# A two-layer recurrent and attention kernel: the start of the first layer put in another order, and its sine computed on GpSimd

## The chip, the cores and the metric

One core of one Trainium2 chip runs the kernel. The metric is the device time in microseconds (us). The kernel before took 806.47 us, the median of 3 runs (805.55 to 806.91). The engines are TensorE (PE), VectorE (DVE), ScalarE (ACT), GpSimd (POOL) and the DMA queues, of which SyncE (SP) issues nearly all. They run side by side and wait for one another on semaphores.

## The reference

The input is 16 sequences of 256 tokens with 256 features. Two layers follow; each is `x + s * silu(f)`, with `s` from a mixing branch and `f` from a feed-forward branch, both of the normalised `x`. All the changed instructions belong to layer 0:

```
xn = layernorm(x)
mag = exp(-exp(softplus(nu_log)));  theta = exp(theta_log)
A = mag * (cos(theta) + i sin(theta));  gamma = sqrt(1 - mag^2)
h[t] = A * h[t-1] + gamma * (xn[t] @ B)          # 32 complex states
s = Re(h @ C) + D * xn
f = gelu(xn @ proj1.T + b1) @ proj2.T + b2       # 256 -> 1024 -> 256
x = x + s * silu(f)
```

Layer 1 has attention with 16 heads in the place of the recurrence, and a linear layer with low-rank experts in the place of the MLP.

## The kernel before

Layer 0 works on 8 chunks of 512 rows (2 sequences). A float32 matmul is made of three products of rounded parts: each operand is split into a high part, written by ScalarE with a Copy (`xh`, `w1h`, `hh`), and the rest, a subtraction on VectorE (`xl`, `w1l`, `hl`). `three` (L505) issues low weight by high data, high weight by low data, high by high.

Every engine runs its own loop over the same steps `g` from 0 to 69, and within a step in the order in which the code stands; nothing is reordered at run time. Step g of TensorE is:

- up(g) (`l0_up`): 6 matmuls of 512 columns, block g % 8 of the hidden layer of chunk g // 8. ScalarE then makes GELU(g) and `hh` (L884), VectorE makes `hl` (`h_low`, L1317).
- down(g-2) (`l0_down`): 12 matmuls of 256 columns. They need `hh` and `hl` of block g-2, and two blocks share one quarter of `w2h` and `w2l`.
- At some steps also: the transposes of the next chunk, 4 matmuls a half (`l0_turn(c, 0)` and `l0_turn(c, 1)`); the input product of the recurrence (`l0_bu`); and its output product (`l0_y(c, b)`), at L777 to L813.

Both halves of the transposes of a chunk go through one bank, so `l0_turn(1, 1)` waits until ScalarE and VectorE have split the first half (L518 to L520: `xth` and `xtl` of 3). VectorE's split of it is `x_low(1, 0)`, which stands at the end of its step.

VectorE has in its steps: the splits of the weights (`w1_low`, `w2_low`), the norm of chunk 1 (`l0_norm(1)`, a generator of which `go` runs some pieces in each step), `magnitude` (from `nu_log` to `mag` and `gamma`: 31 instructions on one column, nearly all dependent; 23 at step 4 ahead of its `hl`, 8 at step 5), the recurrence `scan(c)` (10 instructions), `l0_sum` (adds the bias once all the down products of a chunk are there), `skip` and `states_out`.

GpSimd makes the powers of the rotation: exp(theta), the reduced angles of 1, 2, 4, ..., 128 steps, their sines and cosines, a table `CS` of 256 steps by doubling, and out of it `tci` and `tsi`, which `scan` reads, and `RR`, the signed output matrix that `l0_y` reads. The sines are taken by ScalarE (`angles`, L905), so GpSimd waits for ScalarE and ScalarE for GpSimd.

Of the kernel before, what the change touches and what calls it, by code (L numbers as in the profile page):

```python
# [56 lines left out]
GATE_REST = 9  # L57
L0_STEPS = 70
# [11 lines left out]
    "w1h", "w2h", "bh", "xth", "gelu", "hsh", "sin", "th0", "wrh", "wnh", "wmh", "lbh", "woh",  # L70
# [6 lines left out]
    "clean", "par", "ang", "nu", "tab", "rt", "fill", "rl", "lr", "kr", "kvr", "n", "qq", "nw", "rs", "oc", "kwk", "kwv",  # L77
# [94 lines left out]
def build(nc, x, consts, rows, vecs, w1t, w2t, b1c, bt, ct, nuth, wqn, wkbt, wqr, wkva, wvbt, wo,  # L172
          baset, lorab, loraa, routert, out):
    ctx = ExitStack()
    with ctx:
        SEM = {name: ctx.enter_context(nc.semaphore(name)) for name in SEMAPHORES}

        def sb(name, shape, dt=F32, where=ctx):
            return where.enter_context(nc.sbuf_tensor(name, shape, dt))
# [61 lines left out]
        VEC0 = sb("VEC0", [128, OFF_BB], F32, l0)  # L241
        l0.close()
# [93 lines left out]
        def col(i, n=1):  # L336
            return par[:, i:i + n]
# [164 lines left out]
        def _(e):  # L502
# [255 lines left out]
            for g in range(L0_STEPS):  # L758
# [16 lines left out]
                if g < 8 * NC:  # L775
                    l0_up(g // 8, g % 8)
                if g in (5, 12, 20, 28, 36, 44, 52, 60):  # L777
                    c = (5, 12, 20, 28, 36, 44, 52, 60).index(g)
                    l0_bu(c)
                if g in (10, 14, 22, 30, 38, 46, 54, 62):  # L780
                    c = (10, 14, 22, 30, 38, 46, 54, 62).index(g)
                    l0_y(c, 0)
# [28 lines left out]
                if g in (11, 16, 23, 31, 39, 47, 55, 63):  # L811
                    c = (11, 16, 23, 31, 39, 47, 55, 63).index(g)
                    l0_y(c, 1)  # L813
# [51 lines left out]
        def _(e):  # L865
            w = Waits(e, SEM)

            def w1_high(n):
                sl = slice(256 * n, 256 * n + 256)
                w.wait_ge(f"wu{n}", 16)  # L870
                e.activation(w1h[:, :, sl], st3[:, :, sl], ACT.Copy).then_inc(SEM["w1h"], 1)

            def w2_high(n):
                sl = slice(2 * n, 2 * n + 2)
                w.wait_ge(f"wd{n // 2}", 16)
                e.activation(w2h[:, sl, :], st8[:, sl, :], ACT.Copy).then_inc(SEM["w2h"], 1)
# [27 lines left out]

            def angles():  # L905
                w.wait_ge("ang", 1)
                w.wait_ge("sin", 1)
                e.activation(col(48, 16), col(32, 16), ACT.Sin).then_inc(SEM["sin"], 1)
# [139 lines left out]
            e.activation(col(56), tsn[:, 0:1], ACT.Sin).then_inc(SEM["sin"], 1)  # L1048
# [3 lines left out]
            for g in range(L0_STEPS):  # L1052
# [12 lines left out]
                if g == 3:  # L1065
                    b_high()
                if g == 0:
                    w1_high(1)
                if g == 0:
                    w1_high(2)  # L1070
                if g == 0:
                    w1_high(3)
# [4 lines left out]
                if g == 0:  # L1077
                    angles()
                if g == 1:
                    w2_high(0)  # L1080
                if g == 2:
                    w2_high(1)
                if g == 3:
                    w2_high(2)
                if g == 5:
                    w2_high(3)
# [27 lines left out]
                c, r = divmod(g - 4, 8)  # L1114
                if r == 0 and 0 <= c < NC - 1:
                    x_high(c + 1, 0)
# [58 lines left out]
        def _(e):  # L1175
# [148 lines left out]
            def scan(c):  # L1324

                w.wait_ge("bu", c + 1)
                w.wait_ge("tab", 3)
# [291 lines left out]
            for g in range(L0_STEPS):  # L1619
# [9 lines left out]
                if g == 1:  # L1629
                    w2_low(0)  # L1630
                if g == 2:
                    w2_low(1)
                if g == 3:
                    w2_low(2)
                if g == 6:
                    w2_low(3)
# [8 lines left out]
                if g == 0:  # L1645
                    w1_low(1)
                if g == 0:
                    w1_low(2)
                if g == 0:
                    w1_low(3)  # L1650
                if g in (9, 12, 20, 28, 36, 44, 52, 60):
                    c = (9, 12, 20, 28, 36, 44, 52, 60).index(g)
# [21 lines left out]
                if g == 0:  # L1674
                    norm = l0_norm(1)
                go(norm, 4)
# [14 lines left out]
                c, r = divmod(g - 4, 8)  # L1691
                if r == 0 and 0 <= c < NC - 1:
                    x_low(c + 1, 0)
# [88 lines left out]
        def _(e):  # L1782
# [50 lines left out]

            w.wait_ge("nuth", 16)
# [12 lines left out]
            w.wait_ge("par", done[0])  # L1847
            e.tensor_scalar(ab, r8, 0.5, None, ALU.mult, ALU.bypass).then_inc(SEM["ang"], 1)
# [3 lines left out]
            s8, c8, w8, v8 = col(48, 8), col(56, 8), col(32, 8), col(40, 8)  # L1852
            w.wait_ge("sin", 2)
            tt(c8, c8, c8, ALU.mult)
            ts(c8, c8, -2.0, 1.0, ALU.mult, ALU.add)
            tt(w8, s8, s8, ALU.mult, free=True)
            tt(v8, c8, c8, ALU.mult)
            tt(w8, w8, v8, ALU.add)
            ts(w8, w8, -0.5, 1.5, ALU.mult, ALU.add)
            tt(s8, s8, w8, ALU.mult)  # L1860
            tt(c8, c8, w8, ALU.mult, free=True)
            ts(v8, s8, -1.0, 1.0, ALU.mult, ALU.mult)
# [289 lines left out]
```

## Time and profile before

| | |
|---|---|
| median of 3 runs | 806.47 us |
| the profiled execution's own time | 806.92 us |
| its span (first to last instruction) | 805.1 us |
| PE busy | 785.2 us, 98% |
| DVE, ACT, POOL busy | 700.0, 523.6, 467.9 us |
| mean granted clock of TensorE | 0.991 |

The own time is 1.8 us above the span and 0.45 us above the median. "Busy" of PE counts matmuls that overlap, with modelled ends, so 98% says that it rarely stands still. In a timeline row the first number is the start, the second how long the row's instructions took; a value in brackets is how long the engine was idle before, and what ended that.

### The profile page before, as it was taken

The page shows a single profiled execution, that of the slowest core. Times are in us where ns is not written, and L with a number is a line of the kernel's source. Part 1 is how long each engine was busy: PE and PEld are TensorE (multiplying, and loading weights), DVE is VectorE, ACT ScalarE, POOL GpSimd, SP SyncE. Part 2 cuts the span into 40 slices and gives each one's busy share as a digit, 9 for nine tenths or more (in the row PEclk, how much of TensorE's full clock was granted, in tenths as well). Part 3 has the DMA queues.
Part 4 walks back from the last instruction along what each step waited for, and adds up shares of the span by engine and source line. Part 5 has one row for each costly group of instructions (what it writes and reads, how often), then busy time and mean ns, then how long its engine had stood idle before and what let it go on. Part 6 is the DMA issues. An engine that isn't in the chain of part 4 may idle for free.

```text
span 805.1 us, 23026 instructions
## 1 busy us (share of the span) xinstructions
PE 785.2 (98%) x7912; PEld 719.0 (89%) x7912; DVE 700.0 (87%) x2647; ACT 523.6 (65%) x1612; POOL 467.9 (58%) x1245
## 2 busy tenths in 40 slices
PE   7999999999999899999999999999999999999978
PEld 5988999888889799899989999999899998999957
DVE  6898787887787799899999999989999899998975
ACT  4554454444553687777767777777777777777672
POOL 6833022012334676866768667686776867759653
PEclk9999999999999899999999999999999999999999
DMA  8610012000001322232222322222232223312210
GB/s 305 239 34 1 1 66 67 1 0 2 1 14 28 59 42 46 49 52 53 53 39 44 56 53 53 37 46 49 53 61 36 46 42 57 64 34 48 45 38 29
DMA packets 101333, 41.15 MB, mean 51 GB/s; under 512 B 91744, under 2 KB 98400, under 8 KB 100576
## 3 DMA queue, kind: packets, MB, share of 16 engines
q1 hardware_dynamic: 98896, 38.89, 21.6%
q8 instruction: 63, 1.03, 0.5%
q10 hardware_dynamic: 2320, 0.79, 0.4%
q14 instruction: 54, 0.44, 0.2%
HBM read 14.47 MB, written 4.19 MB: 23 GB/s over the span
## 4 chain that ended last, share of the span: by engine, by line
PE 85%; DVE 5%; POOL 3%; issue 2%; SPq 2%; ACT 1%; DMA 1%; ACTq 0%; POOLq 0%; DVEq 0%
PE bank L507 57%; PE bank L713 11%; PE bank L735 8%; PE bank L706 3%; PE bank L571 1%; SPq L472 1%; PE bank L621 1%; POOL par L1790 1%; PE bank L581 1%; DVE QA L1521 1%; PE bank L524 1%; DMA QT<-QA 1%; DVE SM L1550 1%; DVE PT L1572 1%; SPq L403 1%
## 5 line engine op out<-in xcount | busy, mean ns | idle before, releaser
L1004 ACT ACTIVATE SM<-SM,stb 128x32 f32<-128x32 f32 (+7 forms) x512 | 206.1, 404 | 65.5 <-DVE stb L1550 62.1
L1951 POOL TENSOR_SCALAR SM<-SM,stb 128x32 f32<-128x32 f32 (+7 forms) x512 | 195.5, 400 | 79.4 <-DVE stb L1557 77.8
L507 PE MATMUL bank<-yh,wq_lo 128*128 128x256 f32 x512 | 151.4, 296 | 0.2 <-DVE QA L1521 0.2
L507 PE MATMUL bank<-yh,wq_hi 128*128 128x256 f32 x512 | 145.2, 284 | 0.0
L507 PE MATMUL bank<-yl,wq_hi 128*128 128x256 f32 x512 | 145.2, 284 | 0.0
L713 PE MATMUL bank<-KT,QT 128*128 128x192 f32 (+4 forms) x640 | 120.7, 327 | 1.7 <-DVE stb L1550 1.7
L1550 DVE CUSTOM_DVE_ANT_0 SM<-bank,CONST 128x224 f32<-128x224 f32 (+3 forms) x320 | 97.0, 346 | 22.4 <-PE bank L713 19.7
L713 PEld LDWEIGHTS bank<-KT,QT 128*128 128x128 f32 x640 | 97.6, 190 | 5.1 <-DVE stb L1550 3.4
L1572 DVE STREAM_TRANSPOSE PT<-SM 128x128 f32<-128x128 f32 (+2 forms) x232 | 99.4, 459 | 3.0 <-PE bank L735 2.7
L507 PEld LDWEIGHTS bank<-yh,wq_lo 128*128 128x128 f32 x512 | 97.7, 191 | 1.9 <-DVE QA L1521 0.4
L507 PEld LDWEIGHTS bank<-yl,wq_hi 128*128 128x128 f32 x512 | 97.7, 191 | 0.0
L507 PEld LDWEIGHTS bank<-yh,wq_hi 128*128 128x128 f32 x512 | 97.7, 191 | 0.0
L1004 ACT ACTIVATION_READ_ACCUMULATOR SM<-SM,stb 128x1 f32 x512 | 96.1, 188 | 0.0
L889 ACT ACTIVATE hs<-bank,B 128x512 f32<-128x512 f32 x64 | 43.9, 686 | 73.4 <-PE bank L507 68.1
L1944 POOL TENSOR_TENSOR QA<-QA 128x256 f32<-128x256 f32 x64 | 48.1, 751 | 71.2 <-DVE QA L1521 71.2
L1521 DVE TENSOR_TENSOR QA<-bank,TR 128x512 f32<-128x512 f32 x128 | 81.9, 681 | 4.5 <-DMA QT<-QA 3.8
L976 ACT ACTIVATE QT<-bank 64x512 f32<-64x512 f32 x128 | 75.3, 588 | 6.5 <-PE bank L507 5.0
L507 PE MATMUL bank<-woe_hi,ol 128*128 128x256 f32 x256 | 75.4, 295 | 0.6 <-DVE ol L1594 0.6
L507 PE MATMUL bank<-w2h,hl 128*128 128x256 f32 x256 | 74.3, 290 | 0.5 <-DVE w2l L1293 0.5
L507 PE MATMUL bank<-w2h,hh 128*128 128x256 f32 x256 | 72.3, 283 | 0.0
L507 PE MATMUL bank<-w2l,hh 128*128 128x256 f32 x256 | 72.3, 283 | 0.0
L507 PE MATMUL bank<-woe_hi,oh 128*128 128x256 f32 x256 | 72.1, 282 | 0.0
(215 smaller groups left out, 2081.0 us busy)
## 6 DMA issues: line engine op xcount, KB each, us to landing
QT<-QA SPq DMA_DIRECT2D x248, 64.0 KB, 2.1
PT<-KV SPq DMA_DIRECT2D x256, 16.0 KB, 1.8
out<-fo SPq DMA_DIRECT2D x32, 128.0 KB, 2.0
X<-in_x SPq DMA_DIRECT2D x7, 512.0 KB, 10.9
stage<-in_wqn SPq DMA_DIRECT2D x2, 1024.0 KB, 9.7
stage<-in_wo SPq DMA_DIRECT2D x2, 1024.0 KB, 5.0
stage<-in_w1t SPq DMA_DIRECT2D x4, 256.0 KB, 5.3
stage<-in_w2t SPq DMA_DIRECT2D x2, 512.0 KB, 6.6
```

What stands on the lines that cost most here:

```text
L507: i = e.matmul(dst, a, b, start=(first and j == 0), stop=(last and j == 2), skip_group_check=skip)
L706: j = e.matmul(sbank[n % 2][32 * i:32 * i + 32, at:to], KT[b % 3][:, p, 32 * kb:32 * kb + 32], Q[:, :, kb:3, i, :], start=True, stop=True)
L713: j = e.matmul(sbank[n % 2][:, at], Q[:, q, :, :].rearrange("p h c -> p (h c)"), KT[b % 3][:, p, 0:32 * q + 32], start=True, stop=True)
L735: j = e.matmul(sums[64 * half:64 * half + 64, :, 32 * q:32 * end], C[rows_, kb // 2, at], PT[rows_, 2 * half:2 * half + 2, kb, q:end, :], ...
L889: e.activation(hs[g % 2][:, :], fbank[g % 2][:, :], ACT.Gelu, bias=B1[:, g % 8:g % 8 + 1]).then_inc(SEM["gelu"], 1)
L976: i = e.activation(QT[r, (2 * b + g // 2) % 3, p, :, g % 2:4:2, :].rearrange("p n j c -> p j n c"), src[r, :, :, :], ACT.Copy)
L1004: i = e.activation(M[:, at], M[:, at], ACT.Exp, bias=S[:, 0, j:j + 1], scale=-1.0, accum_out=S[:, 1, j:j + 1])
L1521: i = e.tensor_tensor(QA[:, part, :, :, g % 2, :], src, TR[:, part, :].rearrange("p (n c) -> p n c", n=8).unsqueeze(1).broadcast_to([128, ...
L1550: i = e.tensor_tensor_reduce(M[:, at], bk[:, at], mask[:, 224 - 32 * q:256], 1.0, 3e38, ALU.add, ALU.min, S[:, 0, j:j + 1])
L1572: return e.transpose(PT[:, slot, 0:k, q:q + some, :].rearrange("p k q c -> p q k c"), src)
L1944: e.tensor_tensor(A[:, 0, 0, :, :], A[:, 0, 0, :, :], A[:, 1, 1, :, :], ALU.subtract)
L1951: i = e.tensor_scalar(P[:, at], P[:, at], S[:, 2, j:j + 1], 1.0, ALU.mult, ALU.mult)
```

## The change

1. The Sin activation is gone from ScalarE. In its place GpSimd evaluates a polynomial (of degree 6 in the square of the half angle, for sine and cosine in one tile `trig`). ScalarE's first activation is a GELU on one column, whose result is not used.
2. `RR` is signed after `tci` and `tsi`; the scan waits for 2 tables, and `l0_y` for all 3.
3. The first up product, `l0_first`, has its four products with `xh` first and those with `xl` last.
4. The splits of w1's later quarters move from step 0 to steps 0, 2 and 4, those of w2 from steps 1, 2, 3, 5 (6 on VectorE) to 1, 3, 5, 6; the split of B on ScalarE moves from step 3 to 4.
5. The norm of chunk 1 starts at step 2 and ends at step 4 (it was step 0 to 2); the first half of chunk 1 is transposed and split at step 5 and no longer at 4.
6. The recurrence of chunk 0 moves from step 9 to 10 on VectorE (its output products on TensorE from 10 and 11 to 11 and 12); that of chunk 1 from 12 to 13 (14 to 15).

```diff
+TURN_FIRST = (5, 12, 20, 28, 36, 44, 52)
+            def l0_first():
+                sl = slice(0, 128)
+                w.wait_ge("w1h", 1)
+                w.wait_ge("w1l", 1)
+                for k in range(2):
+                    w.wait_ge("xth", k + 1)
+                    e.matmul(fbank[0][:, :], w1l[:, k, sl], xh[0][:, k, :], start=(k == 0), stop=False)
+                    e.matmul(fbank[0][:, :], w1h[:, k, sl], xh[0][:, k, :], start=False, stop=False)
+                for k in range(2):
+                    w.wait_ge("xtl", k + 1)
+                    i = e.matmul(fbank[0][:, :], w1h[:, k, sl], xl[0][:, k, :], start=False, stop=(k == 1))
+                i.then_inc(SEM["f1"], 1)
...
             def l0_y(c, b):
+                w.wait_ge("tab", 3)
                 w.wait_ge("zz", 2 * c + b + 1)
...
-                if g in (5, 12, 20, 28, 36, 44, 52, 60):
+                if g in (5, 13, 20, 28, 36, 44, 52, 60):
                     l0_bu(c)
-                if g in (10, 14, 22, 30, 38, 46, 54, 62):
+                if g in (11, 15, 22, 30, 38, 46, 54, 62):
                     l0_y(c, 0)
...
-            e.activation(col(56), tsn[:, 0:1], ACT.Sin).then_inc(SEM["sin"], 1)
+            e.activation(trig[:, 15, 0:1], tsn[:, 0:1], ACT.Gelu)
...
-                if g == 0:
-                    angles()
...
-                w.wait_ge("tab", 3)
+                w.wait_ge("tab", 2)
...
-                if g in (9, 12, 20, 28, 36, 44, 52, 60):
+                if g in (10, 13, 20, 28, 36, 44, 52, 60):
                     go(make)
                     scan(c)
...
-                if g == 0:
+                if g == 2:
                     norm = l0_norm(1)
-                go(norm, 4)
+                go(norm, {2: 1, 3: 4}.get(g, 9))
...
-                c, r = divmod(g - 4, 8)
-                if r == 0 and 0 <= c < NC - 1:
+                if g in TURN_FIRST:
+                    c = TURN_FIRST.index(g)
                     x_low(c + 1, 0)
...
+            s8, c8, v8 = col(48, 8), col(56, 8), col(40, 8)
+            ts(ab, r8, 0.5, None, ALU.mult)
+            both = ab.unsqueeze(1).broadcast_to([128, 2, 8])
+            tt(q1.rearrange("p (i n) -> p i n", i=2), both, both, ALU.mult)
+            tt(SUMS[:, 0:3, :], ODD, q1.unsqueeze(1).broadcast_to([128, 3, 16]), ALU.mult)
+            tt(q2, q1, q1, ALU.mult, free=True)
+            tt(SUMS[:, 0:3, :], SUMS[:, 0:3, :], EVEN, ALU.add)
+            tt(q4, q2, q2, ALU.mult, free=True)
+            tt(PAIRS, SUMS[:, 1:4:2, :], q2.unsqueeze(1).broadcast_to([128, 2, 16]), ALU.mult)
+            tt(PAIRS, PAIRS, SUMS[:, 0:3:2, :], ALU.add)
+            tt(q1, PAIRS[:, 1, :], q4, ALU.mult)
+            tt(q1, q1, PAIRS[:, 0, :], ALU.add)
+            tt(r8, r8, q1[:, 0:8], ALU.mult)
+            tt(s8, r8, q1[:, 8:16], ALU.mult)
+            tt(c8, r8, r8, ALU.mult, free=True)
+            ts(c8, c8, -0.5, 1.0, ALU.mult, ALU.add)
+            ts(v8, s8, -1.0, 1.0, ALU.mult, ALU.mult, free=True)
```

TensorE's first up product before, behind the transposes (`xh0` and `xl0` are the parts of chunk 0, `w1h` and `w1l` those of the weight):

```order
L524 MATMUL bank<-CONST,xn0 128x128 x8
L507 MATMUL bank<-xh0,w1l 128x512
L507 MATMUL bank<-xl0,w1h 128x512
L507 MATMUL bank<-xh0,w1h 128x512
L507 MATMUL bank<-xh0,w1l 128x512
L507 MATMUL bank<-xl0,w1h 128x512
L507 MATMUL bank<-xh0,w1h 128x512
```

The same place in the changed kernel:

```order
L527 MATMUL bank<-CONST,xn0 128x128 x8
L539 MATMUL bank<-xh0,w1l 128x512
L540 MATMUL bank<-xh0,w1h 128x512
L539 MATMUL bank<-xh0,w1l 128x512
L540 MATMUL bank<-xh0,w1h 128x512
L543 MATMUL bank<-xl0,w1h 128x512 x2
```

Both products with `xl0` now stand last of the six.

VectorE before, from step 4 (the last `hl` of the first part of `magnitude`) to step 6; `xl1` is the split of chunk 1, the first one `x_low(1, 0)`, the second `x_low(1, 1)`:

```order
L1321 TENSOR_TENSOR hl1<-hs0,hh1 128x512
L1314 TENSOR_TENSOR xl1<-bank,xh1 128x512
L1201 SCALAR_TENSOR_TENSOR par<-par,pari 128x1
L1196 TENSOR_TENSOR par<-par 128x1
L1198 TENSOR_TENSOR par<-par 128x1
L1201 SCALAR_TENSOR_TENSOR par<-par 128x1
L1196 TENSOR_TENSOR par<-par 128x1
L1198 TENSOR_TENSOR par<-par 128x1
L1201 SCALAR_TENSOR_TENSOR par<-par 128x1
L1280 TENSOR_TENSOR par<-par 128x1
L1321 TENSOR_TENSOR hl2<-hs1,hh2 128x512
L1293 TENSOR_TENSOR w2l<-stage1,w2h 128x512
```

The same place in the changed kernel:

```order
L1325 TENSOR_TENSOR hl1<-hs0,hh1 128x512
L1297 TENSOR_TENSOR w2l<-stage1,w2h 128x512
L1205 SCALAR_TENSOR_TENSOR par<-par,pari 128x1
L1200 TENSOR_TENSOR par<-par 128x1
L1202 TENSOR_TENSOR par<-par 128x1
L1205 SCALAR_TENSOR_TENSOR par<-par 128x1
L1200 TENSOR_TENSOR par<-par 128x1
L1202 TENSOR_TENSOR par<-par 128x1
L1205 SCALAR_TENSOR_TENSOR par<-par 128x1
L1284 TENSOR_TENSOR par<-par 128x1
L1325 TENSOR_TENSOR hl2<-hs1,hh2 128x512
L1318 TENSOR_TENSOR xl1<-bank,xh1 128x512
```

`x_low(1, 0)` has gone behind a weight split, the second part of `magnitude` and one more `hl`.

VectorE before, around the first recurrence (`hl2` is the split of block 8, the four `G` and `g3` begin the scan, `z0` is `l0_sum`, `xn0` is `skip`):

```order
L1321 TENSOR_TENSOR hl2<-hs0,hh2 128x512
L1333 TENSOR_TENSOR G<-bank,tci 64x256
L1334 TENSOR_TENSOR G<-bank,tsi 64x256
L1333 TENSOR_TENSOR G<-bank,tci 64x256
L1334 TENSOR_TENSOR G<-bank,tsi 64x256
L1336 TENSOR_TENSOR g3<-G 128x256
L1338 SCALAR_TENSOR_TENSOR gs<-par,g3 128x256
L1344 TENSOR_TENSOR Z0<-gs,CS 64x256
L1345 TENSOR_TENSOR Z0<-gs,CS 64x256
L1344 TENSOR_TENSOR Z1<-gs,CS 64x256
L1345 TENSOR_TENSOR Z1<-gs,CS 64x256
L1369 TENSOR_TENSOR z0<-bank,VEC0 128x512 x2
```

The same place in the changed kernel:

```order
L1325 TENSOR_TENSOR hl2<-hs0,hh2 128x512
L1373 TENSOR_TENSOR z0<-bank,VEC0 128x512 x2
L1325 TENSOR_TENSOR hl0<-hs1,hh0 128x512
L1357 TENSOR_TENSOR xn0<-xn0,VEC0 128x512
L1337 TENSOR_TENSOR G<-bank,tci 64x256
L1338 TENSOR_TENSOR G<-bank,tsi 64x256
L1337 TENSOR_TENSOR G<-bank,tci 64x256
L1338 TENSOR_TENSOR G<-bank,tsi 64x256
L1340 TENSOR_TENSOR g3<-G 128x256
```

`l0_sum`, the `hl` of block 9 and the second `skip` now come ahead of the scan.

## Rows read from the trace of the kernel before

**Rows 1.** The page: busy time of each engine.
```profile
PE 785.2 (98%) x7912; PEld 719.0 (89%) x7912; DVE 700.0 (87%) x2647; ACT 523.6 (65%) x1612; POOL 467.9 (58%) x1245
```

**Rows 2.** The timeline of TensorE: start, length, line, operands, [idle before, releaser].
```profile
11.45 0.47 PE L507 MATMUL bank<-xh,w1l 128*128 128x512 f32 x1 [1.14 <-DVE xl L1314]
...
17.60 0.47 PE L507 MATMUL bank<-xh,w1l 128*128 128x512 f32 x1 [1.59 <-ACT hs L889]
...
28.66 0.39 PE L507 MATMUL bank<-xh,bl 128*128 128x512 f32 x1
...
31.46 0.40 PE L507 MATMUL bank<-xh,w1l 128*128 128x512 f32 x1
...
32.85 0.60 PE L524 MATMUL bank<-CONST,xn 128*128 128x128 f32 x4
...
45.28 1.13 PE L571 MATMUL bank<-RR,Z 128*128 128x256 f32 x4 [0.56 <-DVE Z L1345]
...
62.04 0.63 PE L524 MATMUL bank<-CONST,xn 128*128 128x128 f32 x4 [0.79 <-DVE xl L1314]
```

**Rows 3.** The timeline of ScalarE, start of the first layer.
```profile
15.47 1.28 ACT L889 ACT_TABLE_LOAD   x1
...
17.49 0.63 ACT L893 ACTIVATE hh<-hs 128x512 fp32r<-128x512 f32 x1
```

**Rows 4.** The timeline of VectorE, up to 47 us.
```profile
10.61 1.29 DVE L1314 TENSOR_TENSOR xl<-bank,xh 128x512 fp32r<-128x512 f32 x2 [0.63 <-ACT xh L882]
...
14.48 1.40 DVE L1212 BATCH_NORM_STATS2 st<-X 128x6 f32<-128x256 f32 x4
...
17.20 0.19 DVE L1201 SCALAR_TENSOR_TENSOR rs<-rs,ri 128x4 f32<-128x4 f32 x1
...
18.25 0.69 DVE L1321 TENSOR_TENSOR hl<-hs,hh 128x512 fp32r<-128x512 f32 x1 [0.86 <-ACT hh L893]
...
25.33 0.14 DVE L1245 TENSOR_SCALAR par<-par 128x1 f32<-128x1 f32 x1
...
29.55 0.69 DVE L1321 TENSOR_TENSOR hl<-hs,hh 128x512 fp32r<-128x512 f32 x1
30.16 0.68 DVE L1314 TENSOR_TENSOR xl<-bank,xh 128x512 fp32r<-128x512 f32 x1
...
32.26 0.73 DVE L1321 TENSOR_TENSOR hl<-hs,hh 128x512 fp32r<-128x512 f32 x1
...
41.38 0.41 DVE L1333 TENSOR_TENSOR G<-bank,tci 64x256 f32<-64x256 f32 x1
...
46.15 1.29 DVE L1369 TENSOR_TENSOR z<-bank,VEC 128x512 f32<-128x512 f32 x2
```

**Rows 5.** TensorE's granted clock in stretches: length, busy times, clock (before DMA share), GB/s.
```profile
12.00:15.00 3.00, 3.00 (x8) 2.32 (x7) 2.25 (x5) 0.66 (x2) 2.49 (x7) 0.50 1.06 398
...
275.00:281.40 6.40, 5.78 (x44) 5.34 (x45) 4.29 (x28) 1.44 (x7) 3.14 (x8) 0.50 0.51 97
...
769.50:772.80 3.30, 2.79 (x48) 2.30 (x48) 2.04 (x17) 1.13 (x6) 1.07 (x3) 0.52 0.16 50
16.00:17.60 1.60, 0.01 (x1) 0.03 (x1) 1.22 (x10) 1.56 (x3) 1.13 (x6) 1.00 1.00 415
```

**Rows 6.** The timeline of TensorE at its two longest waits.
```profile
275.62 1.51 PE L706 MATMUL bank<-QT,KT 128*32 128x192 f32 x24 [2.97 <-DVE stb L1550]
...
769.59 2.79 PE L706 MATMUL bank<-QT,KT 128*32 128x192 f32 x48 [2.54 <-DMA QT<-QA]
```

**Rows 7.** The timeline of GpSimd: begin of the sines, one long row, the last table.
```profile
20.74 0.69 POOL L1796 TENSOR_TENSOR par<-par 128x8 f32<-128x8 f32 x1
...
23.09 2.37 POOL L1790 TENSOR_SCALAR par<-par 128x8 f32<-128x8 f32 x1
...
25.99 0.20 POOL L1790 TENSOR_SCALAR par<-par 128x8 f32<-128x8 f32 x1
...
40.37 0.55 POOL L1875 TENSOR_SCALAR tsi<-CS,par,CONST 128x256 f32<-128x256 f32 x1
```

More of the change, by code:

```diff
@@ L1 @@
+import math
 from contextlib import ExitStack
@@ L241, in build @@
         VEC0 = sb("VEC0", [128, OFF_BB], F32, l0)
+        trig = sb("trig", [128, 16, 16], F32, l0)
         l0.close()
@@ L774, in _ @@
                     l1_tk(0, wbank)
-                if g < 8 * NC:
+                if g == 0:
+                    l0_first()
+                elif g < 8 * NC:
                     l0_up(g // 8, g % 8)
-                if g in (5, 12, 20, 28, 36, 44, 52, 60):
-                    c = (5, 12, 20, 28, 36, 44, 52, 60).index(g)
+                if g in (5, 13, 20, 28, 36, 44, 52, 60):
+                    c = (5, 13, 20, 28, 36, 44, 52, 60).index(g)
                     l0_bu(c)
-                if g in (10, 14, 22, 30, 38, 46, 54, 62):
-                    c = (10, 14, 22, 30, 38, 46, 54, 62).index(g)
+                if g in (11, 15, 22, 30, 38, 46, 54, 62):
+                    c = (11, 15, 22, 30, 38, 46, 54, 62).index(g)
                     l0_y(c, 0)
@@ L1064, in _ @@
                     gate_exp(0)
-                if g == 3:
+                if g == 4:
                     b_high()
-                if g == 0:
-                    w1_high(1)
-                if g == 0:
-                    w1_high(2)
-                if g == 0:
-                    w1_high(3)
+                if g in (0, 2, 4):
+                    w1_high(1 + g // 2)
                 if g == 65:
@@ L1076, in _ @@
                     y_high(0, wbank)
-                if g == 0:
-                    angles()
[L1079 to L1086, printed above, removed]
+                if g in (1, 3, 5, 6):
+                    w2_high((1, 3, 5, 6).index(g))
                 if g == 38:
@@ L1112, in _ @@
                     nope_high(1, 1)
-                c, r = divmod(g - 4, 8)
-                if r == 0 and 0 <= c < NC - 1:
+                if g in TURN_FIRST:
+                    c = TURN_FIRST.index(g)
                     x_high(c + 1, 0)
@@ L1628, in _ @@
                     l1_norm(1)
[L1629 to L1636, printed above, removed]
+                if g in (1, 3, 5, 6):
+                    w2_low((1, 3, 5, 6).index(g))
                 if g == 58:
@@ L1644, in _ @@
                     skip(c, 1)
[L1645 to L1650, printed above, removed]
-                if g in (9, 12, 20, 28, 36, 44, 52, 60):
-                    c = (9, 12, 20, 28, 36, 44, 52, 60).index(g)
+                if g in (0, 2, 4):
+                    w1_low(1 + g // 2)
+                if g in (10, 13, 20, 28, 36, 44, 52, 60):
+                    c = (10, 13, 20, 28, 36, 44, 52, 60).index(g)
                     go(make)
@@ L1690, in _ @@
                     h_low(g)
-                c, r = divmod(g - 4, 8)
-                if r == 0 and 0 <= c < NC - 1:
+                if g in TURN_FIRST:
+                    c = TURN_FIRST.index(g)
                     x_low(c + 1, 0)
@@ L1831, in _ @@
             done[0] += 1
+            ODD, EVEN, SUMS, PAIRS = (trig[:, i:i + n, :] for i, n in ((0, 3), (3, 3), (6, 4), (10, 2)))
+            q1, q2, q4 = (trig[:, i, :] for i in (12, 13, 14))
+            for k in range(7):
+                at = SUMS[:, 3, :] if k == 6 else (ODD if k % 2 else EVEN)[:, k // 2, :]
+                e.memset(at[:, 0:8], float((-1) ** k / math.factorial(2 * k + 1)))
+                i = e.memset(at[:, 8:16], float((-1) ** k / math.factorial(2 * k)))
+            i.then_inc(SEM["par"], 1)
+            done[0] += 1
             w.wait_ge("nuth", 16)
```

36 lines of the change are left out of this document (9 added, 27 removed).

## The prediction

> **What bounds the kernel now.** I read the busy time by engine first, then the timelines of the four engines over the first 70 us, since every changed instruction runs there. TensorE is busy for 98% of the span [rows 1], so what follows the start is a belt of matmuls: a microsecond that TensorE gains or loses in its first steps is a microsecond at the end, if nothing gives it back on the way. The reader is to look for TensorE's waits. At the start there are 1.14 us for the low part of x, and 1.59 us for the first GELU at 17.60 [rows 2], which the exchange of ScalarE and GpSimd over the sines had held back: the Sin came first and then a load of the GELU table, 1.28 us [rows 3]. Then TensorE stands twice for VectorE: 0.56 us at 45.28 for the first recurrence, and 0.79 us at 62.04 for the split of chunk 2 [rows 2]. The second thing to see is VectorE. It runs without a gap from 18.25 to 33.5 [rows 4], and runs behind TensorE: TensorE is at the input product of step 5 at 28.66 [rows 2] when VectorE has yet to write a split of step 4, `x_low(1, 0)`, at 30.16 [rows 4]. TensorE needs it at 32.85 [rows 2]. So TensorE's cover there is 32.85 - 30.8 = 2.0 us. That number decides this change.
>
> **The first steps: what is saved.** With the products on `xh` first, TensorE need not wait for `xl`: `xh` is there when VectorE begins its `xl` at 10.61 [rows 4], so the first product starts at 10.65 and not 11.45. The last product waits for the second `xl` (11.90) and ends at 12.35. ScalarE's GELU(0) follows at 12.4, with no Sin and no table load between; before it began at 15.47 + 1.28 = 16.75 [rows 3]. So ScalarE's chain starts 4.3 us earlier. It then has GELU, `hh`, the w2 copy, GELU and `hh`: by rows 3 a GELU takes 0.72 (17.49 less 16.77) and a copy 0.55 to 0.6, so `hh(1)` is there at 12.4 + 2 x 0.72 + 3 x 0.55 = 15.5. TensorE gets ahead by about 3 us: its wait at 17.60 and most of the slow stretch at 12 to 15 go.
>
> **VectorE: what the saved time meets.** From `hl(0)` at 18.25 to the first instruction of `magnitude` at 25.33 it works without a gap for 7.08 us [rows 4]. The new order, from `hl(1)` at 15.5, has three pieces less (`hl(0)` and two w2 splits, 0.61 each by 29.55 to 30.16 [rows 4]) and two w1 splits more (1.22), and the statistics of chunk 1 with the first round of the root, 14.48 to 17.39 = 2.91 us, which before ran in the shadow of the wait for the Sin. That is 7.08 - 1.83 + 1.22 + 2.91 = 9.4 us, and `magnitude` begins at 24.9: only 0.4 us earlier. Its 23 instructions take 29.55 - 25.33 = 4.22 us [rows 4], to 29.1. Then, before, came one `hl` and `x_low(1, 0)`. Now `x_low(1, 0)` stands at step 5, behind `hl` (0.6), a w2 split (0.6), the rest of `magnitude` (30.76 to 32.26 = 1.5, the 30.76 being 30.16 + 0.6 [rows 4]), and another `hl` (0.6): it begins at 32.4 and ends at 33.1.
>
> TensorE, meanwhile, is held at step 5 by the split of B, which ends at 24.9. From there it has the input product and the down product (28.66 to 31.46 = 2.80 [rows 2]), the first transposes (0.35) and up(6) (31.46 to 32.85 = 1.39), and stands before `l0_turn(1, 1)` at 29.45. It waits there for `x_low(1, 0)` until 33.15: **3.7 us idle, and 0.3 us later than before** (32.85). The whole gain of the start is spent. Both ends of this term: if the clock falls as at 12 to 15 [rows 5], up(1) takes 1.2 us longer and `hl(1)` comes 0.65 us later, which makes +0.95; if VectorE's pieces are shorter by what GpSimd's smaller share of blocked reads might save, 0. I take +0.3, as the gap ahead of the first product is now 0.3 us where 1.14 went ahead of the slow stretch.
>
> **The recurrence a step later.** From the transposes to the end of down(7) TensorE has no wait: 43.15 before (0.35 + 1.43 + 3 steps of 2.82 from 32.85), 43.45 now. Before, VectorE filled the time between `hl(8)` and that end with the scan (41.38 to 46.15 [rows 4]). Now `l0_sum`, which needs down(7), stands ahead of it, so VectorE idles from 41.4 to 43.5, whatever the offset: up(8) frees its `hl` 2.1 us after its end, down(7) ends 4.25 us after it. Then two sums, an `hl` and a `skip` (4 x 0.6 = 2.4) to 45.9, and the scan gives its first product 45.28 - 41.38 = 3.9 us later [rows 2, 4]: 49.8. TensorE arrives, after up(10), down(8) and up(11), at 43.45 + 4.2 = 47.65 and waits 2.15 us. The same work (up(11) and the first output product) was done at 49.1 before, at 50.55 now: +1.45. A part comes back, since VectorE then sets the pace: it has 7.2 us of work (six instructions at 0.6, the norm of chunk 2 at 1.3, the rotary weights' split at 2.3) from the scan's end (50.7) to the sum of states that frees the bank of `l0_bu(1)`, 57.9, where TensorE waits some 0.4 us; the 0.79 us at 62.04 (1.1 if one goes by the starts of rows, as the 0.56 is 0.75; ends of matmuls are modelled) is gone, because `x_low(2, 0)` is now early. Net over the stretch: 2.15 + 0.4 - 0.75 - 1.1 = +0.7; with rounding of the starts I put **+0.6**. From below this is 0 (VectorE catches up in its later gaps), from above 1.45.
>
> **The clock.** Here the trace of before is the witness. After 2.97 us and after 2.54 us idle [rows 6] TensorE resumed at a granted clock of 0.50, which is 1.2 and not 2.4 GHz, and kept it until 281.4 and 772.8 [rows 5]: 5.8 and 3.2 us of work at half speed. After 1.14 us idle, with gaps ahead of that, 3.2 us were at half (12.0 to 15.2); after 1.59 us none (1.00 at 16.00:17.60 and after). A wait of 3.7 us is longer than any of these, so I expect 3.2 to 5.8 us at half speed behind it, a loss of 1.6 to 2.9 us. Two of the three rows say the smaller: **+1.6**. It is on the path: down(7) comes later by as much.
>
> **GpSimd.** The 14 memsets run while it waits for its first input. One instruction fewer ahead of `magnitude`'s input, 15 where 9 were for the sines: 6 more at 0.3 us is +1.8, less the 0.3, and `RR` behind `tci` and `tsi` gives 0.5 back. The last table that the scan needs was ready at 40.92 [rows 7]; now at about 41.9. The scan starts at 45.9, so this costs nothing; the cover is 4 us. What GpSimd shows of contention: a row of 8 columns takes 0.20 us at 25.99 but 2.37 us from 23.09 to 25.46 [rows 7], while VectorE ran `hl`, split, `hl`, split.
> The Trainium skill (SBUF — State Buffer, "Who interferes with whom") says that a VectorE instruction with two SBUF inputs blocks a GpSimd instruction that reads SBUF for its whole length; this row agrees. By that rule each of the six extra instructions could meet such a run; that is the rival of the late table below. By the rule as by the row the sum stays as it is until 4 us of cover are used up.
>
> **Sum.** 0.3 + 0.6 + 1.6 = +2.5 us on 806.92, the profiled execution's own time: 809.4. The median of the runs is 0.45 below that execution, so 809.0 for the median. Its own range: 0 + 0 + 1.6 to 0.95 + 1.45 + 2.9, which is +1.6 to +5.3, 808.0 to 811.8.
>
> **Rivals.**
> 1. *The waits come, the clock does not fall.* For it: 1.59 us idle left the clock at 1.00. Against: both waits above 2.5 us lowered it. Time: +0.9, 807.4. Chance 22%.
> 2. *Faster: the start's gain gets through.* One mechanism: `x_low(1, 0)` ends before TensorE stands at the second transposes. Then TensorE goes on at 29.5, not 32.85: -3.4, and +0.6 for the scan: -2.8, 803.7. It decides when VectorE is 3.6 us ahead of my sum at that place; any lead below 0.3 us gives nothing. Against it: 17.6 us of packed VectorE work whose pieces all have rows. For it: I may misplace a wait of VectorE in the old order that does not come back in the new one; half the lead would be -1.1 and no fallen clock. Chance 15%, mostly between 803.7 and 805.5.
> 3. *The table becomes the bound.* If GpSimd's sines and doublings take 4 us more than I put, each further microsecond moves the scan and the end. Two blocked rows like that at 23.09 (2.2 us extra each) on top would do it. With 1 us beyond: +3.5, 810.0. Chance 5%.
> My forecast has 58%.
>
> **Chances.** A measurement of this kernel can tell about 0.2%, 1.6 us. Slower by more: the forecast's 58% save its lowest edge, and the late table: 0.60. Within: the first rival and the edges: 0.26. Faster: 0.14. The range leaves out most of the second rival and the top of the third: 805.3 to 811.3.
>
> **What would show it.** In the new profile: ScalarE's first GELU at 12.4 with no table load before it; TensorE's first product at 10.65; `magnitude` at 24.9 and the split `xl` of chunk 1 at 32.4; a TensorE wait of 3 to 4 us that ends at about 33 with transposes, and a granted clock of 0.5 behind it; VectorE idle 2 us before `l0_sum`; a wait of about 2 us at the first output product. The prediction is wrong if `xl` of chunk 1 comes before 31, if no TensorE wait above 1.5 us stands between 20 and 40 us, or if the second table ends after 45.

## The result, and the profile after

The changed kernel takes 809.02 us, the median of 11 runs (807.03 to 813.27), against 806.2 for 11 runs of the kernel before, taken in turns on the same chip: a ratio of 1.004, 95% interval 1.0023 to 1.0058. It is slower by about 3 us. The forecast was 809.0.

The two profiled executions do not show it at first sight. The one of after has a span of 805.2 us and an own time of 807.03, which is the fastest of its 11 runs; the one of before has 805.1 and 806.92. What has to be compared is where each stands on the way, and at which clock. The page's line of the busy engines:

```profile
PE 781.3 (97%) x7912; PEld 715.3 (89%) x7912; DVE 700.8 (87%) x2647; ACT 522.0 (65%) x1610; POOL 467.5 (58%) x1264
```

TensorE is busy 3.9 us less than in [rows 1] in the same span: it stands still more, and runs less at half clock. The mean granted clock is 0.998, before 0.991. Windows of after (start:end, us, busy time and count by engine, granted clock, DMA share, GB/s) over the stretches that answer to [rows 5]:

```profile
12.00:15.00 3.00, 3.00 (x14) 2.36 (x13) 1.55 (x3) 2.40 (x4) 2.41 (x8) 1.00 1.07 392
33.70:39.70 6.00, 5.98 (x40) 5.52 (x41) 3.56 (x6) 1.92 (x3) 5.45 (x13) 1.00 0.64 218
277.90:281.90 4.00, 4.00 (x39) 3.55 (x40) 3.68 (x22) 1.35 (x6) 1.98 (x6) 0.59 0.75 141
```

Before had three slow stretches (12, 275 and 769.5); this execution has one, at 278. The timeline of TensorE (start, duration, line, operation, count; in brackets how long it had stood and for whom) answers to [rows 2]:

```profile
10.72 0.47 PE L539 MATMUL bank<-xh,w1l 128*128 128x512 f32 x1 [0.34 <-ACT xh L903]
15.46 0.36 PE L510 MATMUL bank<-w2h,hl 128*128 128x256 f32 x1 [0.20 <-DVE w2l L1297]
25.52 0.47 PE L510 MATMUL bank<-xh,bl 128*128 128x512 f32 x1 [1.36 <-DVE bl L1303]
33.72 0.63 PE L527 MATMUL bank<-CONST,xn 128*128 128x128 f32 x4 [3.32 <-DVE xl L1318]
50.68 1.10 PE L590 MATMUL bank<-RR,Z 128*128 128x256 f32 x4 [2.23 <-DVE Z L1349]
58.89 0.50 PE L510 MATMUL bank<-xh,bl 128*128 128x512 f32 x1 [0.18 <-DVE xn L1364]
71.57 1.02 PE L590 MATMUL bank<-RR,Z 128*128 128x256 f32 x4
```

The last row is the last output product of chunk 1, a place that comes behind everything that was moved. The kernel before is there 1.99 us earlier. Its first down product and that last output product:

```profile
19.69 0.36 PE L507 MATMUL bank<-w2h,hl 128*128 128x256 f32 x1 [0.46 <-DVE w2l L1293]
69.58 1.02 PE L571 MATMUL bank<-RR,Z 128*128 128x256 f32 x4
```

The first down product is at 15.46 where it was at 19.69, so the start did bring 4.2 us. It is all gone at 33.72: there the kernel before, at 32.85, is ahead by 0.87. VectorE shows why (answering to [rows 4]):

```profile
15.78 0.71 DVE L1325 TENSOR_TENSOR hl<-hs,hh 128x512 fp32r<-128x512 f32 x1 [0.46 <-ACT hh L914]
25.29 0.15 DVE L1249 TENSOR_SCALAR par<-par 128x1 f32<-128x1 f32 x1
32.89 0.68 DVE L1318 TENSOR_TENSOR xl<-bank,xh 128x512 fp32r<-128x512 f32 x1
44.28 1.29 DVE L1373 TENSOR_TENSOR z<-bank,VEC 128x512 f32<-128x512 f32 x2 [2.11 <-PE bank L510]
46.69 0.41 DVE L1337 TENSOR_TENSOR G<-bank,tci 64x256 f32<-64x256 f32 x1
```

From 15.78 to 33.5 no row of it shows a gap, and `magnitude` begins at 25.29, as before (25.33). ScalarE, in its timeline, has the load of the table at 1.18 us, where it hides behind the input's transfer, and GELU(0) at 12.56 where it was 16.77:

```profile
1.18 1.28 ACT L1064 ACT_TABLE_LOAD   x1 [1.18 <-PEq L2147]
12.56 0.69 ACT L910 ACTIVATE hs<-bank,B 128x512 f32<-128x512 f32 x1 [0.99 <-PE bank L543]
```

GpSimd, in its own timeline, has a group of 8 polynomial instructions (3.06 us from 22.39; the last of them is the first row here) and the second table of the recurrence; the table is ready at 41.48:

```profile
24.89 0.56 POOL L1790 TENSOR_TENSOR trig<-trig 128x16 f32<-128x16 f32 x1
40.93 0.55 POOL L1881 TENSOR_SCALAR tsi<-CS,par,CONST 128x256 f32<-128x256 f32 x1
```

### The profile page after: what moved, and what is told of

Same layout as the page of the kernel before. It is cut to its first block, busy times and chain, and to the rows that moved or that the text cites. A ratio compares the mean times of both kernels' runs of the same rounds, so it can differ in the third digit from the quotient of the medians.

```text
span 805.2 us, 23043 instructions
## 1 busy us (share of the span) xinstructions
PE 781.3 (97%) x7912; PEld 715.3 (89%) x7912; DVE 700.8 (87%) x2647; ACT 522.0 (65%) x1610; POOL 467.5 (58%) x1264
## 4 chain that ended last, share of the span: by engine, by line
PE 84%; DVE 7%; issue 2%; SPq 2%; POOL 1%; DMA 1%; ACT 1%; ACTq 0%; POOLq 0%; DVEq 0%
PE bank L510 57%; PE bank L732 11%; PE bank L754 8%; PE bank L725 3%; PE bank L590 2%; SPq L475 1%; PE bank L600 1%; PE bank L640 1%; DVE QA L1525 1%; DMA QT<-QA 1%; PE bank L527 1%; DVE SM L1554 1%; DVE PT L1576 1%; SPq L406 1%; PE bank L614 1%
```

## The experiments

Every kernel below was timed in turns with the kernel before, which stood at 805.95, 805.96 and 805.84 us (26, 35 and 35 runs) in the three sets of four (experiments 1 to 4, 5 to 8, 9 to 12), each set on another chip. "The mark" is the last output product of chunk 1 (69.58 before, 71.57 after).

**1. The changed kernel again**, for a second profile.

> The changed kernel itself, beside the others on one chip. The theory (two VectorE-bound waits at the start, 3.3 us ahead of the second transposes of chunk 1 and 2.2 us ahead of the first output product): the same two waits, TensorE 2.0 us later than before at the last output product of chunk 1 (71.6 against 69.6), and 809 us where before has 806 to 806.5. The rival (the difference of 2.8 us between the medians was a matter of when TensorE's clock fell in single executions): no difference to before in these rounds.

809.56 us, ratio 1.0053 (1.0037 to 1.007). Same code, same wait, another clock:

```profile
33.71 1.09 PE L527 MATMUL bank<-CONST,xn 128*128 128x128 f32 x4 [3.31 <-DVE xl L1318]
53.31 2.05 PE L590 MATMUL bank<-RR,Z 128*128 128x256 f32 x4 [2.23 <-DVE Z L1349]
75.28 1.02 PE L590 MATMUL bank<-RR,Z 128*128 128x256 f32 x4
```

```profile
33.70:39.70 6.00, 5.99 (x23) 5.48 (x24) 2.45 (x4) 0.60 (x1) 5.46 (x12) 0.51 0.63 218
53.40:56.60 3.20, 3.20 (x11) 2.84 (x12) 3.16 (x8) 0.00 (x0) 0.00 (x0) 0.50 0.00 0
```

In six microseconds TensorE gets 23 matmuls done instead of 40, and after the second wait it is slow again. The mark comes 3.7 us later than in the first profile. So the same program can lose 3.7 us on its first 75, or nothing.

**2. First transposes at step 4 again.**

```diff
-TURN_FIRST = (5, 12, 20, 28, 36, 44, 52)
+TURN_FIRST = (4, 12, 20, 28, 36, 44, 52)
```

> The changed kernel with only the first transposes and the split of chunk 1 back at step 4. The theory: TensorE then waits for the norm of chunk 1 at its first transposes (until 25.0, some 4 us), and the second transposes find the split there: they begin at about 32.4 and not 33.7, so the end comes 1.3 us sooner, 807.7. Rival (it is VectorE's total work up to that point that sets the time, wherever the split stands): unchanged, 809.

807.9 us, 1.0031 (1.0017 to 1.0045), where 807.7 was expected and the rival had 809. The long wait moved and did not go:

```profile
25.30 1.11 PE L527 MATMUL bank<-CONST,xn 128*128 128x128 f32 x4 [3.81 <-DVE xn L1229]
35.51 0.60 PE L527 MATMUL bank<-CONST,xn 128*128 128x128 f32 x4
52.43 1.10 PE L590 MATMUL bank<-RR,Z 128*128 128x256 f32 x4 [2.23 <-DVE Z L1349]
```

TensorE now stands for the norm of chunk 1 and not for its split, and the clock was at half from 24.3 to 31.9. The second transposes have no wait. The work from the first transposes to the end of the next up product takes 6.01 us here (25.30 to 31.31) and 3.25 in the kernel before (25.41 to 28.66), so half clock cost 2.8 us. Without it, as an estimate, the second transposes would stand at 32.7 and the mark at 70.6, 1.0 us ahead of the changed kernel. So the place of the split is worth about 1 us; the rest of the wait is VectorE's work ahead of the norm, wherever the transposes stand.

**3. The recurrence of chunk 0 at step 9 again.**

```diff
-                if g in (10, 13, 20, 28, 36, 44, 52, 60):
+                if g in (9, 13, 20, 28, 36, 44, 52, 60):
...
```

(and its output products at 10 and 11, on TensorE and VectorE alike)

> The changed kernel with only the first recurrence back at step 9 (its output products at 10 and 11). The theory: VectorE no longer idles 2.1 us before the bias sum, the scan starts at 42.2 behind the split of block 8 (the tables are there at 41.5), the wait at the first output product falls from 2.2 to about 0.6 us, and the last output product of chunk 1 comes 1.1 us sooner: 807.9. Rival (the table is the bound, which is why the scan was moved): the scan starts later than 43 and nothing is gained.

806.84 us, 1.002 (1.0007 to 1.0033), 2.7 us under the changed kernel in the same set. The second wait is gone:

```profile
33.68 0.63 PE L527 MATMUL bank<-CONST,xn 128*128 128x128 f32 x4 [3.32 <-DVE xl L1318]
47.60 1.10 PE L590 MATMUL bank<-RR,Z 128*128 128x256 f32 x4 [0.48 <-DVE Z L1349]
70.84 1.02 PE L590 MATMUL bank<-RR,Z 128*128 128x256 f32 x4
```

The clock was at half from 35 to 38.8 here, so the mark says too little; experiment 9 has it clean. The gain is more than double what I had expected (1.1).

**4. `magnitude` two steps later**, so that the split of chunk 1 comes ahead of it.

```diff
-                if g == 4:
+                if g == 6:
                     make = magnitude()
```

> The changed kernel with magnitude started at step 6 in place of 4, so that the split of chunk 1 does not stand behind it. The theory: no wait of TensorE at the second transposes, which begin at 30.3; the whole 3.4 us of the start reach the end, less what the clock does: 805.6 to 806. Rival (the 31 small instructions only move, and VectorE lacks the same 5.7 us a little later): at the first output product TensorE waits for what it gained, 809.

806.69 us, 1.0019 (1.0005 to 1.0032), where 805.6 to 806 was expected.

```profile
30.31 0.60 PE L527 MATMUL bank<-CONST,xn 128*128 128x128 f32 x4
48.07 2.04 PE L590 MATMUL bank<-RR,Z 128*128 128x256 f32 x4 [3.06 <-DVE Z L1349]
70.88 1.02 PE L590 MATMUL bank<-RR,Z 128*128 128x256 f32 x4
```

The transposes start 3.4 us earlier and without a wait: taking the 31 small instructions (4.2 and 1.5 us) from ahead of `x_low(1, 0)` is enough to end it. But the next wait grows from 2.23 to 3.06, which is 0.8 us, and the clock behind it is at half: from the first output product to the next transposes it is 5.33 us (48.07 to 53.40), where the changed kernel's first profile has 3.76 (50.68 to 54.44). At the mark 0.7 us is left of the 3.4. GpSimd's part in the wait, in its timeline (the last of the group of 8, and the second table):

```profile
24.98 2.37 POOL L1790 TENSOR_TENSOR trig<-trig 128x16 f32<-128x16 f32 x1
43.01 0.98 POOL L1881 TENSOR_SCALAR tsi<-CS,par,CONST 128x256 f32<-128x256 f32 x1
```

The table is ready 2.5 us later (43.99 where it was 41.48), and the recurrence starts at 44.07. Most of it is one instruction of 16 columns: it starts at 24.98 and takes 2.37 us, where the changed kernel has 24.89 and 0.56. VectorE now runs the split of B, `hl`, a split and `hl` back to back beside it (25.04 to 27.26), and it ends at 27.35. In the changed kernel instructions on one column follow the split of B, which ends at 25.37, and GpSimd's ends at 25.45.

**5. Unused matmuls in both waits**, of 512 columns each into a bank that nothing reads, 13 ahead of the second transposes and 8 ahead of the first output product, so that TensorE does not stand.

```diff
+                if (c, k) == (1, 1):
+                    for i in range(13):
+                        e.matmul(wbank[:, :], w1h[:, 0, 0:128], xh[0][:, 0, :], start=True, stop=True)
...
```

> The changed kernel with 13 matmuls of 512 columns into an unused bank ahead of the wait at the second transposes, and 8 ahead of the wait at the first output product; their results are used by nothing. They fill 2.8 of the 3.3 us and 1.7 of the 2.2 us. The forecast's theory (the clock falls behind the long wait in most executions and costs about 1.6 us): the median falls by 1 to 1.6 us against the changed kernel, to 807.5 to 808, and the mean granted clock rises. Rival (the clock does not fall there; the waits cost their own length only): the same median, 809.

807.68 us, 1.0019 (1.0004 to 1.0034), 1.9 us under the changed kernel in experiment 1; the mean granted clock over its 12 runs is 0.9966, over all 17 of the changed kernel 0.9942.

```profile
33.74 0.63 PE L530 MATMUL bank<-CONST,xn 128*128 128x128 f32 x4 [0.38 <-DVE xl L1324]
50.70 1.10 PE L596 MATMUL bank<-RR,Z 128*128 128x256 f32 x4 [0.42 <-DVE Z L1355]
71.61 1.02 PE L596 MATMUL bank<-RR,Z 128*128 128x256 f32 x4
```

The useful work is where it was to 0.04 us, and the granted clock was 1.00 over the first 70 us. What is left of the distance to the kernel before (1.7 us) is what the order of the work costs; what is gone fits the clock's share.

**6. Edits 3 and 4 together.**

> Both: magnitude at step 6 and the first recurrence at step 9. The theory: with TensorE 3.4 us ahead the tables (41.5) are the bound, the scan starts at 41.6 and not at 38.7, blocks the bias sum and the split behind it, and TensorE waits 3 us at the first output product; that is 0.9 us worse than magnitude at step 6 with the scan at 10, so about 806.7. Rival (the scan at 9 is better in any case, as with the changed kernel's start): 1 us better, 804.8.

808.17 us, 1.0029 (1.0015 to 1.0044): worse than either alone.

```profile
46.89 1.78 PE L590 MATMUL bank<-RR,Z 128*128 128x256 f32 x4 [4.76 <-DVE Z L1349]
71.70 1.02 PE L590 MATMUL bank<-RR,Z 128*128 128x256 f32 x4
```

With the recurrence early and its table late (ready at 42.80), VectorE stands 2.53 us at the table with two sums and an `hl` queued behind, and the wait is 4.76 us, followed by half clock from 47 to 50.7. The late table of the one edit meets the early recurrence of the other; I had the direction of that and not its size (806.7).

**7. The kernel before with the new sines alone** (`RR` last and the GELU table first go with them).

```diff
-                e.activation(col(48, 16), col(32, 16), ACT.Sin).then_inc(SEM["sin"], 1)
-            e.activation(col(56), tsn[:, 0:1], ACT.Sin).then_inc(SEM["sin"], 1)
+            e.activation(trig[:, 15, 0:1], tsn[:, 0:1], ACT.Gelu)
```

> The kernel before with the sines on GpSimd, the GELU table loaded at the start and RR signed last; all orders of before. The theory: GELU(0) at 13.8, the first split of VectorE at 17.4 behind the statistics of chunk 1 and not at 18.25, TensorE 0.85 us ahead until step 9; the scan then waits for the table (41.5) and TensorE for the scan, so almost nothing is left: 806.0, same. Rival (the exchange with ScalarE was the real cost at the start): 2 us faster, 804.3.

807.32 us, 1.0018 (1.0003 to 1.0033), 1.3 over the expectation. Its first down product is 0.4 us earlier than before's, its second transposes 0.4 us (32.44), and then:

```profile
45.97 1.10 PE L590 MATMUL bank<-RR,Z 128*128 128x256 f32 x4 [1.66 <-DVE Z L1349]
```

```profile
41.97 0.42 DVE L1337 TENSOR_TENSOR G<-bank,tci 64x256 f32<-64x256 f32 x1 [0.98 <-POOL tsi L1883]
```

Taking 1.28 us of table load off ScalarE brings nothing, since VectorE sets the pace there; and with the recurrence in its old place GpSimd's table is on the path, 0.98 us late (second fence, VectorE's timeline). At the mark it is 0.6 us behind the kernel before (70.18). This is the one use of moving the recurrence to step 10.

**8. The same with `l0_first`.**

> The same, and the first product in its new order. The theory: VectorE's first split still comes at 17.4, so TensorE's 0.8 us earlier start is hidden, same as the kernel without it, 806.0; only a clock that stays up at 12 to 15 could show, and that stretch lies in the shadow of VectorE. Rival: 0.8 us faster than the kernel with the sines alone.

806.54 us, 1.0008 (0.9997 to 1.0019): no difference from before. It is 0.8 us under experiment 7, as the rival had it, but the two intervals overlap, so that gain is not shown.

```profile
15.69 0.47 PE L510 MATMUL bank<-xh,w1l 128*128 128x512 f32 x1 [1.70 <-DVE w1l L1292]
20.02 0.55 PE L510 MATMUL bank<-w2h,hl 128*128 128x256 f32 x1 [2.71 <-DVE w2l L1299]
```

The first product is at 10.80, 0.65 us early, and the lead is lost at once for the splits of w1 and w2, which stand in the old order. Behind the 2.71 us the granted clock was 0.53 from 20.0 to 23.4.

**9. Edit 3 with the 13 unused matmuls of edit 5** (the recurrence at step 9, the wait at the second transposes filled; the 8 matmuls of edit 5 are not in it).

> The changed kernel with the first recurrence back at step 9 and 13 matmuls, used by nothing, in the wait at the second transposes. The theory (each wait costs its length, and the long one costs the clock besides): the recurrence at 9 without a fallen clock, 1 to 1.5 us below the kernel with the recurrence at 9 alone (806.8), so 805.6. Rival (the fill of both waits gained 1.9 us at the second wait only, which is small here): 806.8 again.

806.95 us, 1.002 (1.0002 to 1.0038): 1.3 us over the expectation, and no better than experiment 3. Its 12 times fall into two groups: six from 804.9 to 805.7 with mean granted clocks of 0.995 to 0.998, and six from 808.2 to 809.5 with 0.992 to 0.994. The median lies where no run is.

```profile
33.77 0.63 PE L530 MATMUL bank<-CONST,xn 128*128 128x128 f32 x4 [0.39 <-DVE xl L1321]
46.13 1.10 PE L593 MATMUL bank<-RR,Z 128*128 128x256 f32 x4 [0.45 <-DVE Z L1352]
69.37 1.02 PE L593 MATMUL bank<-RR,Z 128*128 128x256 f32 x4
```

At the mark it is 2.2 us ahead of the changed kernel and 0.2 ahead of the kernel before. Its profile has slow stretches later on, at 275 to 279 and 770 to 776, in code that no edit touches; the kernel before has such stretches at the same two places [rows 5].

**10. `magnitude` in two parts**: 3 pieces at step 4, none at step 5, the rest later.

```diff
-                go(make, 7)
+                go(make, {4: 3, 5: 0}.get(g, 7))
```

> The changed kernel with magnitude in three parts: 3 pieces at step 4, none at 5, the rest from 6. The split of chunk 1 comes at 29.7, TensorE does not wait at the second transposes (30.3), and VectorE's two-input instructions are less bunched than with magnitude at 6, so the tables are ready by 42.5 and not 44. The theory: first output product at 47.3 (48.1 with magnitude at 6), wait 2.3 us, last output product of chunk 1 at about 69.5 with the clock up; median 806.0. Rival (GpSimd's tables and its roots for chunk 2 are the bound once TensorE is 3 us ahead, whatever VectorE's order): the output product at 48, 806.7 as with magnitude at 6.

805.73 us, 1.0003 (0.9987 to 1.0019): the best variant, equal to the kernel before. The second transposes start at 30.19 without a wait, the table is ready at 41.85, and the profile's clock is 1.00 throughout:

```profile
47.37 1.10 PE L590 MATMUL bank<-RR,Z 128*128 128x256 f32 x4 [2.50 <-DVE Z L1349]
69.90 1.02 PE L590 MATMUL bank<-RR,Z 128*128 128x256 f32 x4
275.89 0.86 PE L725 MATMUL bank<-QT,KT 128*32 128x192 f32 x24 [2.97 <-DVE stb L1554]
```

```profile
275.30:282.80 7.50, 6.91 (x75) 6.75 (x76) 7.12 (x46) 5.08 (x25) 3.12 (x8) 1.00 0.45 85
```

**11. Experiment 10 with 8 unused matmuls ahead of the first output product.**

```diff
+                if (c, b) == (0, 0):
+                    for i in range(8):
...
```

> The same with 8 matmuls, used by nothing, ahead of the first output product. The theory: no slow stretch at 47 to 51, 1 to 1.5 us less in the median than without, 804.8, below both kernels. Rival (that wait is too short to matter): 806.

808.11 us, 1.0031 (1.0014 to 1.0047), over 3 us above the expectation.

```profile
47.34 1.10 PE L593 MATMUL bank<-RR,Z 128*128 128x256 f32 x4 [0.68 <-DVE Z L1352]
69.87 1.02 PE L593 MATMUL bank<-RR,Z 128*128 128x256 f32 x4
276.00 1.51 PE L728 MATMUL bank<-QT,KT 128*32 128x192 f32 x24 [2.97 <-DVE stb L1557]
```

```profile
275.30:282.80 7.50, 6.80 (x50) 6.35 (x51) 5.00 (x30) 2.46 (x10) 3.19 (x8) 0.54 0.44 84
```

The mark is where experiment 10 has it, to 0.03 us. Then both meet the same wait of 2.97 us at 276, and one goes on at full clock with 75 matmuls in 7.5 us, the other with 50. I have no reason for it in the first 70 us. Nor does the clock account for the 2.4 us between the medians: the mean granted clocks of the two sets of 12 runs are 0.9954 and 0.9947, and 0.0007 of the span is 0.6 us. The rest is open.

**12. Experiment 11 with GpSimd's rotary tables behind the roots for the norm of chunk 2.** In experiment 11 VectorE stood 1.54 us for these roots, and TensorE 1.12 us, at 52.4, for the norm.

```diff
+                if g == 8:
+                    w.wait_ge("const", 16)
+                    for q in range(2):
...
+                    i.then_inc(SEM["rt"], 1)
```

> The same, and GpSimd's rotary tables made behind the roots of chunk 2 and not ahead of them, so those roots are ready 1.4 us earlier. The theory: VectorE does not wait for them before the norm of chunk 2 (1.8 us with magnitude at 6), 0.5 us less, 804.3. Rival (that wait has cover in TensorE): the same as without.

806.53 us, 1.0013 (0.9996 to 1.0031), 2.2 us over the expectation.

```profile
68.38 1.02 PE L593 MATMUL bank<-RR,Z 128*128 128x256 f32 x4
768.14 2.79 PE L728 MATMUL bank<-QT,KT 128*32 128x192 f32 x48 [3.09 <-DMA QT<-QA]
```

At the mark it is 1.2 us ahead of the kernel before and 3.2 ahead of the changed one; the median is 0.7 above before. Late in the run, at the second row, it is still 1.45 us ahead (before: 769.59 [rows 6]). Then the clock is at 0.55 from 768 to 778.5, where before has half clock for 3.3 us, and the profile ends 1.9 us behind. No variant beat the kernel before by more than its interval.

## Why the prediction was right, step by step

**The start's gain is spent at the second transposes: right in mechanism, too small.** Forecast: first product at 10.65, GELU(0) at 12.4, `magnitude` at 24.9, the split of chunk 1 at 32.4, TensorE released at 33.15. Measured: 10.72, 12.56, 25.29, 32.89, 33.72. The wait is 3.32 us where I put 3.7. The term is +0.87 where I put +0.3, inside its bounds (0 to 0.95). `hl(1)` is at 15.78 and not 15.5, which is half of it; the rest is about 0.1 us in each of VectorE's packed stretches. Experiment 4 shows the cause by taking it away: without the 31 small instructions ahead the transposes start at 30.31. Experiment 10, which leaves 12 of them there, has 30.19. No run moves the later norm or the weight splits back alone, so what each of them adds to VectorE's packed work is argued from its rows and not shown.

**The scan a step later: mis-sized.** The wait at the first output product is 2.23 us (forecast 2.15), VectorE's idle time ahead of the sum 2.11 (2.1), and the later wait 0.18 (0.4). The net was to be +0.6 and is +1.12: 71.57 - 69.58 = 1.99, less 0.87. The step that failed is a subtraction in mixed measures: I took the two waits of before by the starts of rows (0.75 and 1.1) and those of after in the rows' own measure. In one measure it is 2.23 + 0.18 - 0.56 - 0.79 = +1.06. Experiments 3 and 9 say what this edit costs inside the new order: 2.7 us by the medians (experiment 3 against 1), 2.2 at the mark (9 against the profile after). That is double the 1.1: between the second transposes and the mark, step 9 in the new order is 1.1 us faster than step 9 in the old one (the other edits gain that much there), and the move to step 10 costs 2.2 from that.

**The clock: size about right, and not a fixed event.** Forecast: behind the wait of 3.7 us half clock for 3.2 to 5.8 us, +1.6. In the first profile the clock stayed at 1.00 behind 3.32 us; in the second it fell behind 3.31, and the mark was 3.7 us later. Over the 13 profiles that are not of the kernel before, TensorE had a wait of 2.7 us or more in the first 70 us seven times, and the clock was at half during it or just behind it in six; the exception is the first profile of after. The share in the median I can only estimate: each run's record has its mean granted clock, and a straight line of time over clock gives at full clock 806.4 for the 17 runs of after and 804.0 for the 96 of before (803.6 to 804.5 by set), a difference of 2.4. That is near the 1.99 of the mark. The mean of all 17 runs of after is 809.6, that of before 806.0; 3.6 less 2.0 to 2.4 leaves 1.2 to 1.6 us. The mean clocks themselves, 0.9942 and 0.9952, are only 0.001 apart, which is 0.8 us of the span. The estimate holds only if a part of before's half clock falls where TensorE waits anyway; the stretch at 12 to 15, ahead of its wait at 17.60, may be such a part, but no run measures it. Experiment 5 is the better witness: it takes 1.9 us away by filling the waits, with the useful work in place and a higher mean clock.

But experiments 9 and 11 filled a wait too and gained nothing, or lost, and their mean clocks are no higher for it (0.9951 against 0.9948 in experiment 3, 0.9947 against 0.9954 in experiment 10). The slow stretches at 275 and 770 are not theirs alone: behind the wait of 2.97 us at 275 to 281 the clock fell in 13 of all 14 profiles, before among them, and around 770, behind waits of 1.7 to 3.5 us, in 8. That it is chance which execution has them, and not the edit's doing, is not shown.

**GpSimd's table costs nothing: right.** It was ready at 41.48, forecast 41.9, needed at 46.69. The cover was real, though: at the old place of the scan it was 0.98 us late (experiment 7). The long row of [rows 7] comes again in experiment 4, as one instruction of 16 columns: 2.37 us there, 0.56 in the changed kernel. It ends 0.09 us after the last of four packed VectorE instructions in the one and 0.08 us after a single one in the other. The Trainium skill (SBUF — State Buffer, "Who interferes with whom") has a VectorE instruction with two SBUF inputs hold up GpSimd's reads for its length; the 1.8 us between these two rows agree with it, though here one GpSimd instruction stood through four of them, and no run varied VectorE's inputs alone.

**The rivals.** *Waits without a fallen clock* (807.4) is what the one profiled execution shows, with own time 807.03; the median of 11 is not there. *The start's gain gets through* (803.7) needed VectorE 3.6 us earlier at the split; experiment 4 gave it that, and still the median was 806.69: in its profile the next wait took 0.8 of the 3.4 us and the half clock behind it 1.6. That rival was priced too high even on its own condition. *The late table* did not come.

So the forecast of +2.5 is the order's 0.9 and the clock's 1.6. Measured it is 2.0 for the order, and 2.8 (medians of the first 11 runs) to 3.6 (means of all) in total. The two waits and the half clock behind them were forecast rightly, and the sum is inside its range on its merits; that 809.0 was met to 0.02 us is luck. The order was put 1.1 us too low (0.6 at the second transposes, 0.5 behind them, where the subtraction in mixed measures stands), the clock's 1.6 lies between the 0.8 that the first 11 medians leave for it (2.8 less 2.0) and the 1.9 of experiment 5, and the sum was set on 806.47, where more runs gave 806.0.

## What to carry to other kernels

When engines run fixed step orders, a lead is worth only what the next engine in the loop can follow: list the work that stands packed ahead of the instruction the bottleneck waits for, and count small dependent instructions by time (23 of them were 4.2 us here) before moving anything past them. Compare two profiles at a mark behind all moved work and at the same granted clock, in one measure of waiting for both; equal spans can hide 2 us, as they do here. If waits differ, take several profiles of the same kernel before a clock effect of a microsecond or two is put down to an edit.

## What the runs showed of the hardware that I had not expected

- The granted clock behind a wait is not settled by the wait's length. The same 3.3 us at 33.7 was followed by full clock in one execution and by 6 us at 0.51 in another; the same 2.97 us at 276 by 1.00 in experiment 10 and 0.54 in experiment 11.
- Over all 14 profiles the 2.97 us at 275 to 281 was followed by half clock 13 times; experiment 10 is the one exception.
- Shorter waits can do it too: behind 2.23 us the clock was at 0.50 for 3.2 us in experiment 1, and at 1.00 behind the same wait in the first profile of after.
- One program's runs spread over 6 us (807.03 to 813.27 for after, 803.52 to 809.84 for before), more than any edit here was worth. The pairs of profiles above differ by such stretches and by little else.
- The same GpSimd instruction on 16 columns took 0.56 us with one VectorE split beside it and 2.37 us with four packed ones.
